# A twelve-stage transformer kernel: where the semaphores of a finished stage are cleared

## The reference

```python
x = x + 0.5 * _L0_ffn_ref(_layernorm(x, axis=-1), L0_ffn_weight)
x = x + _L0_attn_ref(_layernorm(x, axis=-1), L0_attn_W_w, L0_attn_W_b, L0_attn_out_w, L0_attn_out_b)
x = x + 0.5 * _L0_ffn_ref(_layernorm(x, axis=-1), L0_ffn_weight)
x = x + 0.5 * _L1_ffn_ref(...)     # 16 gated experts, top 2, plus a shared one
x = x + _L1_attn_ref(...)          # four Mamba (state space) layers
x = x + 0.5 * _L1_ffn_ref(...)
x = x + 0.5 * _L2_ffn_ref(...)     # 16 GELU experts, top 4
x = x + _L2_attn_ref(...)          # linear and window attention, gated
x = x + 0.5 * _L2_ffn_ref(...)
x = x + 0.5 * _L3_ffn_ref(...)     # quantised linear layers with LoRA
x = x + _L3_attn_ref(...)          # squared-ReLU attention
x = x + 0.5 * _L3_ffn_ref(...)
```

## Time and profile before

| what | value |
|---|---|
| median of 3 runs | 2748.93 us (2746.9 to 2752.26) |
| the profiled execution, its own time | 2750.35 us |
| span of its instructions | 2748.6 us |
| mean granted TensorE clock, share of full speed | 0.959 |
| instructions | 37972 |

### The profile page before, as it was taken

One profiled execution on the slowest core, in us unless ns is written; L12 is line 12 of the kernel. 1 busy time (PEld: TensorE's weight loads), 2 busy tenths in 40 slices (PEclk: granted clock), 3 DMA queues, 4 the chain that ended last, 5 costly groups with the idle time before them and its releaser, 6 DMA issues. The chain is left out here.

```text
span 2748.6 us, 37972 instructions
## 1 busy us (share of the span) xinstructions
PE 2499.3 (91%) x11190; PEld 1421.5 (52%) x11190; DVE 1939.4 (71%) x3923; ACT 1620.2 (59%) x3505; POOL 1144.2 (42%) x919
## 2 busy tenths in 40 slices
PE   7999978689999999999988899978879998799977
PEld 5766743345555555555434344446644445556655
DVE  6888856399999999999955444356644444587754
ACT  3565522388888888888832344357753443466634
POOL 1000011189999999999930000042310001355432
PEclk9999989899999999999999999979989998999988
DMA  2000023234444444444433112000002110000000
GB/s 105 1 1 1 1 85 74 82 136 157 163 161 154 170 160 164 155 164 160 169 133 81 47 62 96 28 1 1 0 21 89 62 62 27 1 1 0 1 1 16
DMA packets 34618, 205.63 MB, mean 75 GB/s; under 512 B 4000, under 2 KB 5152, under 8 KB 13216
## 3 DMA queue, kind: packets, MB, share of 16 engines
q1 hardware_dynamic: 34464, 203.83, 20.7%
HBM read 201.19 MB, written 2.62 MB: 74 GB/s over the span
## 5 line engine op out<-in xcount | busy, mean ns | idle before, releaser
L1313 POOL TENSOR_TENSOR mam_state_c<-mam_state,weights_r 128x1024 f32<-128x1024 f32 x256 | 599.9, 2362 | 16.1 <-DVE mam_state L1246 15.0
L1246 DVE TENSOR_TENSOR_SCAN mam_state<-banks,mam_dbu 128x1024 f32<-128x1024 f32 x256 | 577.1, 2275 | 1.6 <-ACT banks L1392 0.6
L1496 PE MATMUL banks<-mam_state_c,identity 128*128 128x512 f32 x1024 | 485.1, 607 | 12.3 <-POOL mam_state_c L1313 11.3
L1392 ACT ACTIVATE banks<-mam_dt,mam_a_neg 128x255 f32<-128x255 f32 x1024 | 425.0, 461 | 66.4 <-DVE mam_state L1246 65.9
L1496 PEld LDWEIGHTS banks<-mam_state_c,identity 128*128 128x128 f32 x1024 | 187.1, 190 | 226.1 <-issue 190.6
L1005 PE MATMUL banks<-route_xnt,weights_r 128*128 128x512 f32 x512 | 247.6, 608 | 8.1 <-PEq L69 8.1
L1229 DVE TENSOR_TENSOR mam_dbu<-banks,weights_r 128x1024 f32<-128x1024 f32 x192 | 227.5, 1198 | 8.3 <-ACT banks L1400 8.3
L558 POOL TENSOR_SCALAR route_ln_rs<-route_ln_mv 128x4 f32<-128x4 f32 x16 | 5.1, 316 | 494.6 <-DVE route_ln_mv L636 494.6
L438 ACT ACTIVATE at_probs<-banks,at_nmax 128x256 f32<-128x256 f32 x256 | 117.7, 471 | 138.0 <-DVE at_nmax L379 138.0
L2512 POOL TENSOR_TENSOR at_attention<-at_relu 128x512 f32<-128x512 f32 x128 | 131.0, 1040 | 128.0 <-ACT at_relu L2557 86.5
L959 DVE TENSOR_TENSOR m2b_hidden<-m2b_gelu,m2b_comb_spread 128x512 f32<-128x512 f32 x120 | 80.7, 690 | 116.4 <-ACT m2b_gelu L985 113.7
(11 more groups left out here) (434 smaller groups left out, 5031.9 us busy)
## 6 DMA issues: line engine op xcount, KB each, us to landing
weights_r<-mam_bc_rows SPq DMA_DIRECT2D x128, 1024.0 KB, 4.7
m2a_comb_spread<-m2a_comb_rows SPq DMA_DIRECT2D x15, 1024.0 KB, 8.2
m2b_comb_spread<-m2b_comb_rows SPq DMA_DIRECT2D x15, 1024.0 KB, 7.1
m1a_comb_spread<-m1a_comb_rows SPq DMA_DIRECT2D x14, 512.0 KB, 7.2
m1b_comb_spread<-m1b_comb_rows SPq DMA_DIRECT2D x14, 512.0 KB, 7.2
weights_r<-in_mb SPq DMA_DIRECT2D x1, 4332.0 KB, 13.0
weights_r<-in_m SPq DMA_DIRECT2D x1, 4200.0 KB, 12.8
weights_r<-in_a SPq DMA_DIRECT2D x1, 2632.0 KB, 12.1
```

The lines of the kernel that those rows point to most:

```text
L1246: dve.tensor_tensor_scan(flat2(h[:, i % 4, :, :, :]), decay(i), flat2(dbu[:, i % 4, :, :, :]), 0.0, ALU.mult, ALU.add).then_inc(h_ready, 1)
L1313: pool.tensor_tensor(hc[:, j % 4, :, :, :], h[:, j % 4, :, :, :], c_rows(j), ALU.mult).then_inc(hc_ready, 1)
L1392: i = act.activation(decay(j)[:, o + 1:o + S], dt[:, q, c, 1:S], ACT.Exp, scale=aneg[:, l, k:k + 1])
L1496: k = pe.matmul(y_bank(q)[:, :], K.ident[:, :], flat(hc[:, j % 4, n, :, :]), start=(j == 0 and n == 0), stop=(j == NP - 1 and n == 1))
```

## The change

`clear_sems`, with its block, is gone. `retire_sems` takes its place: it instructs no engine, but gives back the semaphore numbers of the stage before, which have been cleared by then, and keeps the list of the stage that has just ended as `K.retired`. The next stage takes its semaphores while those are still held, so it has others. In its block `start_loads` makes the sync engine clear the retired ones ahead of everything else that it does there. What f3b used is not cleared by the program any more.

```diff
-def clear_sems(K):
-    with K.nc.Block() as block:
-        @block.sync
-        def _(sp):
-            for sem in K.live_sems:
-                sp.sem_clear(sem)
-    K.live_sems = []
-    K.sem_scope.close()
+def retire_sems(K):
+    K.retired_scope.close()
+    K.retired, K.retired_scope = K.live_sems, K.sem_scope
+    K.live_sems, K.sem_scope = [], ExitStack()
...
-        K.sem_scope = ctx.enter_context(ExitStack())
-        K.live_sems = []
+        K.sem_scope, K.retired_scope = ExitStack(), ExitStack()
+        K.live_sems, K.retired = [], []
...
         def start_loads(block, tag):
+            if K.retired:
+                @block.sync
+                def _(sp):
+                    for sem in K.retired:
+                        sp.sem_clear(sem)
             due = [p for p in used if LOAD_AT.get(p) == tag]
...
             STAGES[tag][0](K, tag)
-            clear_sems(K)
+            retire_sems(K)
```

## The result

The changed kernel takes 2728.0 us (median of 5 runs, 2726.56 to 2735.28); the kernel before, in the runs that went with it, 2750.35 us (5 runs, 2746.9 to 2752.26). The ratio is 0.9921, with a 95% interval of 0.991 to 0.9932: 0.8% faster, clear of the 0.2% that a measurement of this kernel can tell; the interval stands for 18.7 to 24.8 us saved. The forecast was 2726.3 us with a range of 2720 to 2733, or 22.6 us saved.

A forecast was written before the change was run, and what follows sets the result against it. At the seams only the sync engine works, so the clearing blocks are on the path in full: 24.5 - 2.9 (m1b) + 2.7 (m2a clock) - 1.7 (m1b clock) = 22.6 us saved, 2726.3 us, range 2720 to 2733.

The forecast's parts named there:

- The removed blocks: At the twelve stage boundaries: 20.9 us of clears plus 3.6 us of barrier go, 24.5 us saved.
- the 1.1 us of excess at three seams: Three seams last longer than their clears explain, about 1.1 us in the sync engine's list, counted within the 24.5.
- m1b: 51 clears stay ahead of m1b's loads, so VectorE and TensorE wait for the transfer chain: 2.9 us lost.
- The clears, moved: The sync engine's 332 clears run during the next stage and cost nothing, except in m1b.
- the slower rival: Clears beside four working engines hold up their signals; at 0.1 us a clear 33 us lost, 2760 us; chance 0.02.
- point of decision: For the slower case, 332 clears would each have to cost 0.068 us of the path to eat the 22.6.
- TensorE's clock: Shorter idle time at seams changes the granted clock: m2a gains 2.7 us, m2b nothing, m1b loses 1.7.
- The term for m2a: With 1.0 us idle at the seam, m2a's first 5.5 us run at full clock: 2.7 us gained.
- The term for m1b: TensorE's longer wait in m1b brings a half clock, partly falling into the wait: 1.7 us lost.
- m2b was to gain nothing: At m2b's start the half clock stays, since the 2.77 us wait inside at2 just before stays: no gain.
- Code loading: At the seams: code is fetched ahead and a block's end mostly hidden, so nothing is lost on any engine.
- if stages other than m1b grow: A sign in the profile after that the forecast is wrong; all stages but m1b and m2a should keep equal length.

The follow-up runs named there:

- run 6: The kernel before, its clearing blocks kept, but neighbouring semaphore numbers cleared by one instruction: 2725.8 us, ratio to before 0.9914.
- run 4: The changed kernel with the sync engine's clears behind a stage's weight loads in place of ahead of them: 2732.94 us, ratio to before 0.9936.
- run 7: Run 1 with every moved clear made twice, 664 in place of 332: 2720.98 us, ratio to before 0.9894.
- run 9: Run 1 with range clears behind the loads and at2's weights loaded in m2a in place of m1b: 2713.46 us, ratio to before 0.9863.
- run 8: Run 1 with the clearing block ahead of m2a put back, and 12 in place of 14 additional instructions: 2722.55 us, ratio to before 0.9902.
- run 3: The kernel before with 114 additional clears of an unused semaphore on VectorE in f0a: 2769.08 us, ratio to before 1.0067.
- run 5: The changed kernel with neighbouring semaphore numbers cleared by one instruction, 22 clears in place of 332: 2733.31 us, ratio to before 0.9929.
- run 11: The changed kernel once more, unaltered, for a second profile: 2736.91 us.
- run 1: The changed kernel with 14 additional clears of an unused semaphore on VectorE in f0a: 2716.46 us, ratio to before 0.9883.
- run 2: The changed kernel with 7 additional clears of an unused semaphore on VectorE in f0a: 2723.99 us, ratio to before 0.9915.

## Why the prediction came out

**The removed blocks** were forecast at 24.5 us and were 24.35. The way there was right too: run 6 leaves 5.7 us of barriers and single clears where the prediction had 3.6 of barrier, and the number of clears made up the rest. The small misreading in it costs nothing here: of the 1.1 us of excess at three seams, the prediction says that all is in the 24.5, but the 0.3 us ahead of the first clear at 1534 are not.

**m1b** was forecast 2.9 us longer, for the chain of transfers behind the clears, and was 2.9 and 2.8 longer in the two pairs of profiles, with VectorE's wait at 3.95 and 3.79 ("about 4"). Runs 4 and 7 move the chain both ways, by 2.9 us of clears each time, and the end of the wait moves by -3.0 and +3.1. From that end on m1b takes 102.5 to 103.6 us in every profile that has the wait and no later half clock (103.1 before, 102.9 after). So the chain sets m1b's length, and in run 4 it was a late half clock that hid half of the gain. In run 9 it ends long before VectorE needs it, and the first wait left is that for the next pair's chain.

**The clears, moved**, were costed at nothing outside m1b: run 7 shows it, and with it the slower rival is out. Its point of decision was 0.068 us a clear; the doubled clears of m2a, m2b and f3b show less than 0.1 us for 29, 57 and 44 more.

**TensorE's clock** is where a size was off. The term for m2a was 2.7 us; it was 6.1 in one profile and 4.5 in the other. The prediction counted the 5.5 us of half clock at the start and left out a second stretch in the same stage, 6.8 us from 9.0 us on, which went as well in the first profile and shrank to 3.4 in the second. Over the kernels here m2a takes 241.6 us with no half clock, 243.3 with 3.4, 244.7 to 244.9 with 6.5 to 6.8 and 247.6 with 12.5: 0.5 us for each. The term for m1b, 1.7 lost, did not show: the half clock came, as foretold, but fell into the wait. m2b was to gain nothing, and gained 3.4 in one profile and lost 0.5 in the other. Its start is at half clock still, as foretold; what was missing in the first profile was again the later stretch, of 6.8 us. Run 8 and the tally behind it support the cause, idle time at the seam, for the start of m2a. When the later stretches come stays open, and with it m2b's and at3's lengths.

**Code loading** is the step that failed. The prediction put the cost at nothing ("nothing is lost on any engine and the sum stands") and expected all other stages of equal length. It asked whether the clearing blocks had given the engines time to fetch their code, and forgot that taking instructions out of a list moves all that follow. One of its own signs of being wrong, "if stages other than m1b grow", came true in at2. VectorE's loop in at2, 296 instructions, moved by 14 places, and its second and third rounds then fetched code five times each: 8.8 us lost, 8.6 of them in standstills (at2 was 10.5 to 12.0 us longer in runs 3, 4, 5 and 11, which have those places or, run 3, others with the same result; more half clock goes with part of that). Runs 1, 2 and 3 show it from both sides. By the Trainium skill (Runtime: NRT & Kernel Launch, Instruction fetch mechanics) a taken branch whose target is no longer among the fetched pages waits for a fetch; the trace agrees, with VectorE's 2.8 us behind its loop's branch and the ten fetches that the kernel before does not have. The prediction cited an earlier sentence of that section, that the cost of a block's end is mostly hidden, and did not ask about the loops.

So the forecast of 22.6 us was met, 22.35 in the medians and 22.5 in the profiled spans, in part by luck. The blocks and m1b came out as foretold, but the rest, foretold at 1.0 us gained, was the sum of larger terms that cancelled: m2a, m2b and at3 gave 13.5 us in that profile, code placement took 8.8, and seven other stages took 3.8. In the second pair the same terms left 14.4 us saved and not 22.4.

## What to carry to other kernels

Count the clears, not the barriers: a block that clears semaphores one by one costs 0.058 us for each, and one clear over the range of 51 numbers 0.11 us in all. Work that is moved past a barrier onto a queue is free only if nothing that the stage needs stands behind it on that queue; here only one of eleven stages had such a chain. And after any edit that adds or removes instructions ahead of a hardware loop, compare the instruction fetches and the "issue" waits of each loop stage: here somewhere between 7 and 14 places decided whether the body was fetched again in each round, and 7 dummy instructions in idle time bought it back.

## What the runs showed of the hardware

Taking 14 instructions out of VectorE's list made the stage with a later loop of 296 instructions 8.8 to 12.0 us longer over its three rounds, and 7 put back undid it. A clear's record mostly lasts 25 to 30 ns on the sync engine, but the 51 clears in m1b start 57 ns apart; on VectorE the record is 54 ns and they start 84 ns apart. A clear over the 51 numbers of one stage takes 109 to 112 ns, and those over shorter ranges 31 to 89 ns (runs 5 and 6). The granted clock follows the program closely where nothing changes (two profiles of before have the same stretches of half clock to 0.2 us in nearly every stage), while two profiles of the changed kernel differ by 1.3 to 4.1 us in eight stages, so a single pair of profiles cannot price a clock effect of 3 us.
